# Placing the steps that finish the sorted batches at other units beside the last batch's experts

## The reference

```
weights_BSK, indices_BSK = jax.lax.top_k(probs_BSE, TOP_K)
norm_weights_BSK = jax.nn.softmax(weights_BSK, axis=-1)
```

## Time and profile before

| | us |
|---|---|
| median of 3 executions | 1489.52 |
| lowest, highest | 1485.62, 1489.63 |
| the profiled execution's own time | 1500.58 |
| its span, first to last instruction | 1498.6 |
| dense units, first gate product to last down product | about 1385 to 1485 of the span |
| behind the last down product | about 14 |

### The profile page before, as it was taken

One profiled execution on the slowest core, in us unless ns is written; L12 is line 12 of the kernel. 1 busy time (PEld: TensorE's weight loads), 2 busy tenths in 40 slices (PEclk: granted clock), 3 DMA queues, 4 the chain that ended last, 5 costly groups with the idle time before them and its releaser, 6 DMA issues. The chain is left out here.

```text
span 1498.6 us, 45273 instructions
## 1 busy us (share of the span) xinstructions
PE 1404.8 (94%) x17868; PEld 930.3 (62%) x17868; DVE 1215.5 (81%) x2717; ACT 1036.8 (69%) x2010; POOL 1154.2 (77%) x667
## 2 busy tenths in 40 slices
PE   4899999999999999999999999999999999899985
PEld 1366666666666656666666656666666566599764
DVE  7788888888788898888889899888888997765456
ACT  2677777778777877778777767777777676534334
POOL 5588887978787878988787978898879888543464
PEclk8799999999999999999999999999999999999997
DMA  5444444633233324333333323333332252143121
GB/s 169 117 114 142 142 142 123 179 111 97 63 90 84 79 72 108 81 83 81 90 82 94 83 68 97 81 83 79 79 89 61 69 182 62 46 131 90 45 57 55
DMA packets 104081, 142.31 MB, mean 95 GB/s; under 512 B 16960, under 2 KB 51520, under 8 KB 103488
## 3 DMA queue, kind: packets, MB, share of 16 engines
q1 hardware_dynamic: 100800, 133.13, 32.6%
q0 software_dynamic: 3072, 6.30, 1.4%
HBM read 20.49 MB, written 24.38 MB: 30 GB/s over the span
## 5 line engine op out<-in xcount | busy, mean ns | idle before, releaser
L1250 ACT ACTIVATE probs<-psum 128x512 f32<-128x512 f32 x1024 | 614.5, 603 | 251.8 <-PE psum L966 250.9
L2013 POOL TENSOR_TENSOR probs_lo<-probs 128x1024 f16<-128x1024 f32 x299 | 651.3, 2183 | 154.7 <-ACT probs L1250 151.0
L985 PE MATMUL psum<-cv,probs 128*128 128x66 f16 x4096 | 476.3, 193 | 7.8 <-DVE probs_lo L1580 4.8
L987 PE MATMUL psum<-cv,probs 128*128 128x64 f16 x4096 | 475.9, 193 | 0.0
L989 PE MATMUL psum<-cv,probs_lo 128*128 128x66 f16 x4096 | 474.7, 192 | 0.0
L1544 DVE CUSTOM_DVE_ANT_0 scan_out<-psum,ahead 128x512 f16<-128x512 f32 x512 | 346.9, 686 | 131.5 <-PE psum L858 120.0
L987 PEld LDWEIGHTS psum<-cv,probs 128*128 128x128 bf16 x4096 | 380.4, 97 | 110.2 <-issue 2.3
L985 PEld LDWEIGHTS psum<-cv,probs 128*128 128x128 bf16 x4096 | 385.4, 97 | 68.7 <-DVE probs_lo L1580 5.3
L964 PE MATMUL psum<-q_both,k_twice 128*128 128x512 f16 x1024 | 388.4, 379 | 3.5 <-ACT probs L1250 3.2
L966 PE MATMUL psum<-q_max,k_ones 65*128 65x512 f16 x1024 | 390.6, 381 | 0.0
L989 PEld LDWEIGHTS psum<-cv,probs_lo 128*128 128x128 f16 x4096 | 380.0, 98 | 0.0
(11 more groups left out here) (221 smaller groups left out, 1812.0 us busy)
## 6 DMA issues: line engine op xcount, KB each, us to landing
t_swapped<-t_sin SPq DMA_DIRECT2D x248, 128.0 KB, 2.0
k_twice<-qk_hi SPq DMA_DIRECT2D x128, 128.0 KB
slots<-oacc SPq DMA_DIRECT2D x25, 512.0 KB, 3.1
q_lone<-qk_hi SPq DMA_DIRECT2D x64, 128.0 KB, 2.3
q_both<-qk_hi SPq DMA_DIRECT2D x64, 128.0 KB
q_both<-qk_lo SPq DMA_DIRECT2D x64, 128.0 KB
q_max<-qk_hi SPq DMA_DIRECT2D x64, 128.0 KB
k_ones<-qk_lo SPq DMA_DIRECT2D x64, 128.0 KB
```

Source lines behind the costliest of these rows:

```text
L985: pe.matmul(acc, high[:, q * P:(q + 1) * P, 1], v[:, 0:VLO], start=opens, stop=False, skip_group_check=True)
L987: pe.matmul(acc[:, 0:DH], high[:, q * P:(q + 1) * P, 1], v[:, VLO:VW], start=False, stop=False, skip_group_check=True)
L1250: act.activation(probs[s % 4][:, i, :], score_ps[tile % SCORE_BANKS], ACT.Exp, scale=SCALE).then_inc(probs_done, 1)
L2013: pool.tensor_tensor(probs_lo[s % 4][:].rearrange("p a n -> p (a n)"), p, p.bitcast(BF16).rearrange("p (n two) -> p n two", two=2)[:, :, 1 ...
```

## The change

Four settings change. The number and the size of all operations stay. The order on POOL changes in one place: the inverse roots of group 1 come behind gather 46 and not behind gather 41.

```diff
-FIRST_GATHER = 2
+FIRST_GATHER = 3
 FINAL_AT = {
-    "weigh": {0: 7, 1: 12, 2: 17, 3: 22, 6: 27, 7: 32},
-    "sums": {0: 8, 1: 13, 2: 18, 3: 23, 6: 28, 7: 32},
-    "stats": {0: 9, 1: 14, 2: 19, 3: 24, 4: 21, 5: 26, 6: 30, 7: 33, 8: 33},
-    "means": {0: 10, 1: 15, 2: 20, 3: 25, 4: 22, 5: 27, 6: 31, 7: 33, 8: 33},
+    "weigh": {0: 9, 1: 13, 2: 17, 3: 22, 6: 26, 7: 30},
+    "sums": {0: 10, 1: 14, 2: 18, 3: 23, 6: 27, 7: 31},
+    "stats": {0: 11, 1: 15, 2: 19, 3: 24, 4: 21, 5: 26, 6: 28, 7: 32, 8: 33},
+    "means": {0: 12, 1: 16, 2: 20, 3: 25, 4: 22, 5: 27, 6: 29, 7: 33, 8: 33},
     "norm": {0: 20, 1: 21, 2: 30, 3: 29, 4: 31, 5: 33, 6: 33, 7: 35, 8: 34},
     "result": {0: 21, 1: 22, 2: 31, 3: 30, 7: 36, 8: 35}}
-ROOTS_BEHIND = {28: (0,), 41: (1,)}
+ROOTS_BEHIND = {28: (0,), 46: (1,)}
```

## The result

| | before | changed |
|---|---|---|
| median of 20 executions each, us | 1486.06 | 1489.99 |
| lowest, highest | 1483.55, 1494.68 | 1486.88, 1501.29 |
| ratio, 95% interval | 1 | 1.0034 [1.0023, 1.0046] |
| the profiled execution | 1500.58 | 1490.98 |
| its span | 1498.6 | 1487.8 |

The change makes the kernel slower by 0.34%, 5.1 us (3.4 to 6.8). That is 3 us over the forecast of +2.2, and next to the +5.4 of rival 1. The two medians are 3.9 us apart, and 1489.99 lies 1.7 under the 1491.7 forecast, since the median of before is now 3.5 us lower than that of its first three executions (1489.52): by the time alone the forecast looks better than it was.

What follows compares the result with a forecast made beforehand. Attention is TensorE-bound; in the last 115 us pauses accompany long gather runs, and without pauses POOL sets the end. Ring +3.0, DVE +0.5, last run gone -1.3 give +2.2: 1491.7 us, range 1482 to 1497.5.

Steps and rivals of the forecast that it cites:

- rival 1: No pauses in timed runs: activate 31 stands behind part 7's weighing and rows; slower, +5.4 us, 1494.9; chance 0.25.
- 64.8 us without waits: First to last gather on POOL if nothing pauses; the execution before would then take 1484.2 us.
- The sum for the one end: All terms against the profiled execution with its pauses: 0 - 1.3 + 0.45 + 0.5 = -0.4 us.
- the sum for the other: Without pauses, from part 7's rows landing to the add of 31: 6.9 against 1.1, less 0.4, +5.4 us.
- My own sign for this case: Over 85 us or under 78 from combine 4 to combine 31 would show the sum of small terms wrong.
- +0.95 for part 7 and DVE: Cost against the profile with pauses: +0.45 for the ring at unit 30, +0.5 for DVE's sums and statistics.
- rival 2: Runs of gathers pause TensorE, shorter runs pause it less: faster, net -6.2 us, 1483.3; chance 0.24.
- FIRST_GATHER 3: First gather of the stage: value 0, at most +0.6 us; POOL kept a unit closer to TensorE, taken as 0.
- Roots behind 46: POOL's last run of seven gathers goes, -2.6 us; a longer run at units 23 to 25, +1.3; net -1.3.
- The ring of part 7: Unit 30: weighing waits for DVE's result 3, activate 31 behind it; +3.0 us without a pause, +0.45 against the profile.
- The weighings of parts 0, 1 and 6: Moved to units 9, 13, 26, where ACT and DVE have room: value 0, bounds -1 to +1 us.
- The port rule: Engines and DMAs reach SBUF by separate ports, so gathers can't cause the pauses and placing them anew removes none.

Runs made afterwards that it cites:

- e9: Kernel before with only group 1's roots moved, behind gather 44 instead of 41; without pauses, ratio 0.9994 [0.9979, 1.0009] to before.
- e1: Kernel before, unchanged, run again for a second profile; with pauses, before 1507.6 us, ratio 1.0011 [0.9992, 1.0030].
- e5: Changed kernel, unchanged, run again beside before; with pauses, before 1506.4 us, ratio 0.9993 [0.9967, 1.0018].
- e11: Kernel before with only part 7 moved (weigh 30, sums 31, stats 32), second run; without pauses, ratio 1.0037 [1.0020, 1.0054].
- e6: Kernel before with only part 7 moved (weigh 30, sums 31, stats 32); with pauses, ratio 1.0031 [1.0010, 1.0053].
- e7: Kernel before with only group 1's roots moved behind gather 46; with pauses, ratio 0.9972 [0.9952, 0.9992].
- e4: Changed kernel with group 1's roots back behind gather 41 and part 7 back at units 32 and 33; with pauses, ratio 0.9971 [0.9960, 0.9982] to before.
- e12: Kernel before with only group 1's roots moved behind gather 46, second run; without pauses, ratio 1.0021 [1.0006, 1.0036].
- e10: Kernel before with group 1's roots behind gather 44 and FIRST_GATHER 3; without pauses, ratio 1.0011 [0.9994, 1.0027].
- e3: Changed kernel with part 7 back at units 32 (weigh, sums) and 33 (stats); with pauses, ratio 0.9965 [0.9951, 0.9978] to before.
- e8: Kernel before with POOL waiting for all gathers so far to land ahead of every fourth one; with pauses, ratio 0.9993 [0.9974, 1.0012].

## Why the prediction was right in its range and wrong in its middle

*What bounds the kernel.* Right without pauses: POOL's gathers set the end. From the first to the last I had 64.8 us without waits; the changed kernel's profile has 63.7, e9's 63.8. That before would then take 1484.2 came within 2 us: its median is 1486.06, its lowest 1483.55. The readings with pauses took the late silus for a pause of TensorE's chain; TensorE's rows stay on pace at first (e1), so who is held up first was read wrong.

*"I take it that the timed runs have some pauses, but fewer or shorter ones."* This step failed. There is no middle. Before takes about 1487 without pauses or 1507 with them (e1, e5, e9, e11), and its one profile with pauses, of 1500.58 us, stood beside timed executions without. The forecast of +2.2 was made between two sums, and nearly all executions lie near one of the two. The sum for the one end was -0.4, and e5 measured -1.1; the sum for the other was +5.4, and the comparison measured +5.1. I gave 0.25 to the one that held, because I read 11 us between profile and median as a part of a quantity, and not as another condition. My own sign for this case was under 78 us from combine 4 to combine 31; the changed kernel's profile has 69.3, so by that sign the sum of small terms was wrong. That the two sums came so near is in part luck. In the one with pauses no term holds: I had +0.95 for part 7 and DVE, -1.3 for the roots and 0 for the rest, and measured +4.7 alone (e6), -4.2 alone (e7) and -4.4 (e4). In the one without, part 7's term holds (+5.4 against +5.5), but the roots had no term at all and cost 3.1 alone; the sum comes out because the two overlap. The range held because it reached from rival 2 to rival 1.

*FIRST_GATHER 3.* I had 0 to +0.6 for the first gather: it comes 3.77 us behind the combine of unit 2, and with FIRST_GATHER 2 it comes at 3.24 in the first profile, 3.51 in e9 and 4.07 in e12. Right. What the setting is worth in all was not told apart from noise without pauses (e10), nor from the weighings with them (e4).

*Roots behind 46.* "Nobody waits for these roots before the shift at unit 28" is true, and the error was to take the roots for done by then. Without pauses POOL reaches them after unit 28's turn, DVE is held for 3.26 us, and alone that costs +3.1. With pauses the sign was right and the size low: -1.3 against -4.2 alone (e7); on top of the other changes the late roots bring some 0.9, within the noise (e3 against e4).

*The ring of part 7.* Right in its rows: 5.2 from combine 30 to combine 31, and 5.30 in the profile. Alone without pauses +5.4 was the sum and +5.5 the measurement. With pauses I let the last pause hide it, +0.45 and +0.5 for DVE; measured +4.7. The prediction took the 4.75 us between the two combines of the earlier trace rows as cover. It wasn't: the pause comes first and the ring behind it, 8.30 us from combine 30 to combine 31 in e6.

*Why the two don't add.* Alone they cost 5.5 and 3.1, together 5.1. Both hold units 28 to 31 up, and what the roots delay, part 7's rows use to land: in the changed kernel weigh 7 waits 2.00 us, until result 3 and its rows are there at nearly the same time; in e11 it waits 7.25 us for the rows.

*The weighings of parts 0, 1 and 6.* I had 0. They weren't run alone. e4 holds them together with FIRST_GATHER 3, with pauses, and gains 0.29%; which of the two brings it stays open.

*The port rule.* The Trainium skill ("SBUF — State Buffer", section "SBUF: two separate sides") has DMA and engines apart, and rival 1 stood beside it (where the prediction says that the rule's result is the second rival, it should say the first). e8 speaks against reading the pauses as something that the gathers have no part in: in its one profile breaking the runs removes nearly all of them. Whether the ports are what the two share, no run here shows, and the packets of the gathers were no slower in an execution with pauses (mean 244 ns for 4096 bytes in the first profile, 239 in the changed kernel's, 251 in e9's).

*No version that beats both everywhere was found.* With pauses e3 and e7 beat both kernels by 0.3%. Without, nothing tried beats before. Roots behind gather 44 cost nothing there that can be told; whether they gain with pauses wasn't run.

## What to carry to other kernels

A step that an engine can't do yet blocks all that is queued behind it. Before moving a step forward, look up what it waits for, buffers it reuses included, and what of the main chain stands behind it: here a weighing moved up by two units cost about 5 us (4.7 and 5.5), as the last silu was queued behind it. And one profile is one execution: when its own time lies 1% from the median of the timed ones, look for a second condition, make the sum for each, and don't forecast a mean of the two.

## What the runs showed of the hardware

The pauses, which I hadn't expected to be so clear cut. Where they occur, an unbroken run of gathers on POOL, 1.25 us apart, goes with late silus from behind the first four to six gathers on. At first TensorE's rows keep their pace of 2.20 us a unit, and only then do they get gaps (e1, e8). The silu's unexplained waits sum to 12 to 29 us in the profiles with pauses and unbroken runs, in a stage of 87. Runs of at most four, each landed ahead of the next, leave 3.1. Where they don't occur, 48 gathers in 63.7 us, without a wait between them, give no such wait at all. By the times, one and the same program has them in all executions of one group and in hardly any of another, and chip numbers 13 and 15 each have a group of either kind. What differs between the groups, and what in a pause holds up the silu, stays open.
